# A pipelined two-block transformer on one core: the expert table read into registers at once, loads in pieces, and new orders

## What is computed

```python
h = layernorm(x) * (1 + ca) + sa
x = x + ga * attention0(h)                      # softmax(Q K^T / sqrt(128)) V
h = layernorm(x) * (1 + cb) + sb
x = x + gb * fp4_linear(silu(fp4_linear(h, w_gate)) * fp4_linear(h, w_up), w_down)
h = layernorm(x) * (1 + ca1) + sa1
x = x + ga1 * attention1(h)                     # 16 heads, causal
h = layernorm(x) * (1 + cb1) + sb1
logits = h @ gate_w.T; weights = softmax(logits of the 4 experts); top 2, made to sum to 1
y = silu(h @ w1[e]) * (h @ w3[e]) @ w2[e]       # for each chosen expert e
x = x + gb1 * sum of weight[e] * y
```

## Time and profile before

| | |
|---|---|
| median of three runs | 1883.6 us (1878.56 to 1885.53) |
| the profiled execution | 1871.67 us, span 1869.9 us |
| instructions | 39385 |
| ScalarE, GpSimd busy | 753.6 us (40%), 764.6 us (41%) |
| weight loads on TensorE | 1179.5 us (63%) |
| transfers | 291.39 MB, mean 156 GB/s |
| mean granted TensorE clock | 0.88 |

### The profile page before, as it was taken

How to read it: one execution, slowest core, us unless ns; L and a number is a source line. 1 busy time by engine, 2 the same in 40 slices (tenths; PEclk the granted TensorE clock), 3 DMA queues, 4 the chain that set the end, 5 groups by cost and what they waited for, 6 DMA issues and landing times. The chain is left out here.

```text
span 1869.9 us, 39385 instructions
## 1 busy us (share of the span) xinstructions
PE 1493.6 (80%) x11729; PEld 1179.5 (63%) x11729; DVE 1244.7 (67%) x2855; ACT 753.6 (40%) x1627; POOL 764.6 (41%) x1324
## 2 busy tenths in 40 slices
PE   3447777898989898988898988899898888772665
PEld 2334544576767676767676777777676767572654
DVE  5567757595959596967787686868695935241332
ACT  1322635454445453535362636363545342320111
POOL 1000142445454545452626163636354545254332
PEclk7667969898999998999999899999898988785887
DMA  5232312464747473736373655556464746444566
GB/s 189 76 107 78 105 60 91 140 209 118 235 120 233 117 235 107 245 93 186 124 215 135 168 175 162 190 143 203 114 226 110 232 136 217 130 123 129 168 197 190
DMA packets 205191, 291.39 MB, mean 156 GB/s; under 512 B 35840, under 2 KB 167936, under 8 KB 200864
## 3 DMA queue, kind: packets, MB, share of 16 engines
q1 hardware_dynamic: 172176, 251.01, 41.1%
q0 software_dynamic: 25824, 27.74, 7.6%
q10 hardware_dynamic: 7088, 11.29, 1.7%
HBM read 215.26 MB, written 70.91 MB: 153 GB/s over the span
## 5 line engine op out<-in xcount | busy, mean ns | idle before, releaser
L938 POOL DMA_INDIRECT acc<-ys,blk x134 | 219.1, 1635 | 448.7 <-issue 249.2
L1804 PE MATMUL bank<-xs_hi,wring 128*128 128x256 f32 x804 | 272.2, 339 | 68.7 <-DVE mneg L1455 30.6
L1455 DVE TENSOR_REDUCE mneg<-bank 128x2 f32<-128x512 f32 (+1 forms) x384 | 238.1, 682 | 60.2 <-remote 41.5
L1125 ACT ACTIVATE arena<-bank 128x512 f32<-128x512 f32 x384 | 197.9, 601 | 133.9 <-PE bank L1691 132.6
L1820 PE MATMUL y_ps<-wring,h 128*128 128x128 f32 (+1 forms) x1608 | 236.8, 289 | 8.3 <-DVE h L1516 7.5
L1805 PE MATMUL bank<-xs_hi,wring 128*128 128x256 f32 x804 | 239.6, 298 | 0.0
L1806 PE MATMUL bank<-xs_lo,wring 128*128 128x256 f32 x804 | 239.4, 298 | 0.0
L1804 PEld LDWEIGHTS bank<-xs_hi,wring 128*128 128x128 f32 x804 | 165.5, 206 | 100.8 <-issue 38.4
L1820 PEld LDWEIGHTS y_ps<-wring,h 128*128 128x128 f32 (+1 forms) x1608 | 207.5, 196 | 26.6 <-DVE h L1516 8.3
L798 POOL TENSOR_TENSOR rstd_a<-ve_a,mhalf 128x4 f32<-128x4 f32 x48 | 49.3, 1027 | 379.0 <-DVE ve_a L1334 376.5
L1516 DVE TENSOR_TENSOR h<-tt,bank 128x512 f32<-128x512 f32 x201 | 134.6, 681 | 71.3 <-PE bank L1806 66.3
(11 more groups left out here) (249 smaller groups left out, 3028.9 us busy)
## 6 DMA issues: line engine op xcount, KB each, us to landing
wring<-w_all SPq DMA_DIRECT2D x201, 640.0 KB, 6.7
blk<-queue SPq DMA_DIRECT2D x67, 272.0 KB, 2.8
q_stack<-q_rows SPq DMA_DIRECT2D x16, 1024.0 KB, 8.7
k_stack<-k_rows SPq DMA_DIRECT2D x16, 1024.0 KB, 11.0
rows<-mod_rows SPq DMA_DIRECT2D x32, 384.0 KB, 3.8
q_rows<-qk_halves SPq DMA_DIRECT2D x48, 256.0 KB, 5.5
k_rows<-qk_halves SPq DMA_DIRECT2D x48, 256.0 KB, 5.6
w_all<-wring ACTq DMA_DIRECT2D x4, 1536.0 KB, 6.5
```

Source lines behind the costliest of these rows:

```text
L938: send(g.indirect_dma_start(acc, bass.IndirectOffsetOnAxis(ap=blk[:, b, t, IDCOL:IDCOL + 1].bitcast(I32), axis=0), ys[:, b % 2, t, :], Non ...
L1125: frees(a(prob(u, g), ps.bank(use)[:], ACT.Exp, scale=SCALE1), use)
L1455: frees(v.tensor_reduce(dst, ps.bank(use)[:].rearrange("p (h k) -> p h k", k=P if name[0] == "A" else S), AX, ALU.max, negate=True), use)
L1804: mm(dst[:, at], w_hi[:, w], xs_hi[:, b % 2, :], start=True, stop=False)
```

## The change

`blocks(it)` and `weights(it, u)` no longer read the table. A new step of SyncE, `read`, waits for the table, reads its eight entries into registers one after another and then releases the table with a semaphore of its own, `table_read`; `make_table` waits for that and no longer for the landing of the ten kinds of loads. `blocks` loads one block, so its four parts can stand at different places of SyncE's list. `weights` and `blocks` build their addresses from the registers. All five orders and the row of bank uses are made anew; the same steps occur as before, some of them for another lead. Of the orders the new lines are shown, and the old ones of SyncE and GpSimd (the old ones of the others stand above); of `USES` only its first line.

```diff
@@ -80,101 +80,102 @@
 LOOP_AT, LOOPS = 2, 10
 
 
-MOE = ("gate", "up", "down", "swish", "times", "weights", "blocks", "table", "lift", "weigh_rows", "add_rows")
-
-
-USES = [(0, "eg1", "D", 5, 0, 4), (0, "eu0", "D", 6, 0, 5), (1, "OT1", "D", 4, 1, 2), (3, "G0", "D", 3, 3, 1),
...
+MOE = ("gate", "up", "down", "swish", "times", "weights", "read", "blocks", "table", "lift", "weigh_rows", "add_rows")
...
+USES = [(3, "G0", "D", 2, 3, 1), (3, "G1", "D", 6, 3, 2), (3, "U0", "D", 1, 3, 3), (0, "X1", "D", 4, 0, 3),
...
 def sp_order(do):
-    do(4, "load1"), do(0, "blocks"), do(0, "weights", 3), do(2, "store_q"), do(0, "weights", 4), do(2, "store_k")
-    do(0, "weights", 5), do(1, "turn_att"), do(0, "weights", 6), do(0, "weights", 7), do(0, "weights", 8), do(2, "stack")
-    do(0, "weights", 9), do(0, "weights", 10), do(1, "store3"), do(0, "weights", 11), do(2, "load4"), do(2, "stack_max")
-    do(4, "load2"), do(2, "stack_v"), do(2, "load3"), do(1, "weights", 0), do(1, "weights", 1), do(1, "weights", 2)
+    do(4, "load1"), do(1, "load3"), do(0, "read"), do(0, "blocks", 0), do(0, "weights", 0), do(0, "weights", 1)
+    do(0, "blocks", 1), do(0, "weights", 2), do(0, "weights", 3), do(2, "store_q"), do(0, "weights", 4), do(2, "store_k")
+    do(1, "turn_att"), do(0, "blocks", 2), do(0, "weights", 5), do(0, "weights", 6), do(2, "stack"), do(2, "stack_v")
+    do(0, "weights", 7), do(0, "blocks", 3), do(0, "weights", 8), do(0, "weights", 9), do(1, "store3"), do(2, "load4")
+    do(0, "weights", 10), do(2, "stack_max"), do(4, "load2"), do(0, "weights", 11)
 def pool_order(do):
-    do(4, "stats1"), do(0, "add_rows", 0), do(1, "stats4"), do(1, "modulate4"), do(1, "route"), do(0, "add_rows", 1)
-    do(1, "scatter"), do(1, "table"), do(3, "stats3"), do(4, "stats2"), do(0, "add_rows", 2), do(0, "add_rows", 3)
+    do(4, "stats1"), do(1, "stats4"), do(0, "add_rows", 0), do(1, "modulate4"), do(1, "route"), do(1, "scatter")
+    do(3, "stats3"), do(1, "table"), do(4, "stats2"), do(0, "add_rows", 1), do(0, "add_rows", 2), do(0, "add_rows", 3)
 def act_order(do):
...
+    do(3, "gate0", 1), do(0, "lift", 1), do(1, "weigh", 2), do(1, "weigh", 3), do(1, "turn_att"), do(4, "norm1")
+    do(3, "gate0", 2), do(3, "gate0", 3), do(0, "gate", 2), do(4, "turn1"), do(0, "gate", 3), do(2, "value1"), do(1, "norm4")
+    do(0, "lift", 2), do(0, "gate", 4), do(1, "turn4"), do(0, "gate", 5), do(1, "logits"), do(4, "query0"), do(4, "key0")
+    do(0, "gate", 6), do(3, "turn_h", 0), do(3, "turn_h", 1), do(3, "turn_h", 2), do(1, "ranks_out"), do(4, "scores0", 0)
+    do(3, "turn_h", 3), do(4, "scores0", 1), do(2, "carry"), do(0, "gate", 7), do(2, "turn_max"), do(4, "probs0", 0)
+    do(0, "gate", 8), do(0, "lift", 3), do(4, "probs0", 1), do(0, "gate", 9), do(0, "gate", 10), do(3, "norm3"), do(3, "turn3")
+    do(2, "rows", 0), do(2, "rows", 1), do(2, "rows", 2), do(2, "weigh", 0), do(4, "norm2"), do(0, "gate", 11)
+    do(2, "weigh", 1), do(2, "rows", 3), do(2, "rows", 4), do(1, "lift", 0), do(2, "rows", 5), do(3, "query1"), do(3, "key1")
+    do(1, "gate", 0), do(4, "turn2"), do(1, "gate", 1), do(4, "gate0", 0)
 def dve_order(do):
...
+    do(0, "swish", 0), do(4, "stats1"), do(0, "swish", 1), do(3, "gate0", 0), do(3, "gate0", 1), do(3, "up0", 0)
+    do(0, "lift", 1), do(3, "up0", 1), do(3, "quantise_h", 0, 0), do(1, "turn_out", 2), do(0, "times", 0), do(1, "turn_out", 3)
+    do(3, "quantise_h", 0, 1), do(0, "times", 1), do(3, "quantise_h", 0, 2), do(3, "gate0", 2), do(0, "swish", 2)
+    do(3, "gate0", 3), do(3, "up0", 2), do(0, "times", 2), do(1, "add3"), do(1, "stats4"), do(0, "swish", 3), do(3, "up0", 3)
+    do(0, "weigh_rows", 0), do(3, "quantise_h", 1, 0), do(0, "times", 3), do(0, "lift", 2), do(0, "swish", 4)
+    do(3, "quantise_h", 1, 1), do(4, "value0"), do(0, "times", 4), do(1, "logits"), do(0, "swish", 5), do(3, "quantise_h", 1, 2)
+    do(0, "times", 5), do(0, "swish", 6), do(2, "maxima", 0), do(0, "times", 6), do(2, "maxima", 1), do(2, "maxima", 2)
+    do(4, "scores0", 0), do(2, "maxima", 3), do(2, "maxima", 4), do(4, "scores0", 1), do(2, "maxima", 5), do(0, "swish", 7)
+    do(3, "down0"), do(2, "turn_max"), do(0, "weigh_rows", 1), do(0, "lift", 3), do(0, "swish", 8), do(3, "stats3")
+    do(0, "times", 7), do(0, "times", 8), do(0, "swish", 9), do(4, "out0"), do(0, "times", 9), do(0, "swish", 10)
+    do(4, "stats2"), do(0, "weigh_rows", 2), do(0, "times", 10), do(0, "swish", 11), do(4, "modulate2"), do(4, "quantise_x", 0)
+    do(0, "times", 11), do(4, "quantise_x", 1), do(2, "turn_out", 0), do(1, "lift", 0), do(4, "quantise_x", 2)
+    do(2, "turn_out", 1), do(0, "weigh_rows", 3), do(3, "query1"), do(3, "key1")
 def pe_order(do):
...
+    do(3, "gate0", 0), do(3, "gate0", 1), do(3, "up0", 0), do(0, "lift", 1), do(3, "up0", 1), do(1, "weigh", 3)
+    do(1, "turn_out", 2), do(0, "up", 0), do(1, "turn_out", 3), do(0, "up", 1), do(1, "turn_att"), do(3, "gate0", 2)
+    do(3, "gate0", 3), do(0, "gate", 2), do(0, "up", 2), do(3, "up0", 2), do(4, "turn1"), do(0, "down", 0), do(0, "gate", 3)
+    do(3, "up0", 3), do(0, "up", 3), do(2, "value1"), do(0, "down", 1), do(0, "down", 2), do(4, "value0"), do(0, "gate", 4)
+    do(0, "lift", 2), do(4, "key0"), do(0, "up", 4), do(1, "turn4"), do(0, "down", 3), do(0, "gate", 5), do(1, "logits")
+    do(0, "up", 5), do(4, "query0"), do(0, "gate", 6), do(2, "maxima", 0), do(3, "turn_h", 0), do(0, "up", 6)
+    do(2, "maxima", 1), do(3, "turn_h", 1), do(0, "down", 4), do(1, "ranks_in"), do(2, "maxima", 2), do(3, "turn_h", 2)
+    do(4, "scores0", 0), do(2, "maxima", 3), do(4, "scores0", 1), do(2, "maxima", 4), do(3, "turn_h", 3), do(0, "down", 5)
+    do(2, "maxima", 5), do(0, "gate", 7), do(3, "down0"), do(2, "turn_max"), do(4, "probs0", 0), do(0, "gate", 8)
+    do(0, "lift", 3), do(4, "probs0", 1), do(0, "up", 7), do(0, "up", 8), do(4, "out0"), do(0, "gate", 9), do(0, "gate", 10)
+    do(0, "down", 6), do(0, "up", 9), do(0, "down", 7), do(3, "turn3"), do(2, "rows", 0), do(2, "rows", 1), do(0, "down", 8)
+    do(2, "rows", 2), do(0, "up", 10), do(2, "weigh", 0), do(0, "gate", 11), do(2, "weigh", 1), do(2, "rows", 3)
+    do(0, "down", 9), do(2, "rows", 4), do(0, "up", 11), do(2, "turn_out", 0), do(2, "turn_out", 1), do(1, "lift", 0)
+    do(2, "rows", 5), do(0, "down", 10), do(3, "query1"), do(0, "down", 11), do(3, "key1"), do(1, "gate", 0), do(4, "turn2")
+    do(1, "gate", 1), do(2, "weigh", 2)
...
@@ -508,7 +509,7 @@
         place_ready, scattered = signal("place_ready", 1), signal("scattered", 2 * TILES, 16)
         step4 = signal("step4", 19)
 
-        table_ready, step5 = signal("table_ready", 1), signal("step5", 24)
+        table_ready, table_read, step5 = signal("table_ready", 1), signal("table_read", 1), signal("step5", 24)
         blk_loaded = [signal(f"blk_loaded{b}", 1, 16) for b in range(BLOCKS)]
         w_loaded = [signal(f"w_loaded{n}", STEPS // RING, 16) for n in range(RING)]
         xs_ready = signal("xs_ready", BLOCKS)
@@ -655,42 +656,47 @@
                 sp.wait_ge(x3_ready.sem, x3_ready.at(it, 1))
                 send(sp.dma_start(acc_v[bass.ds(it.scaled(1), 1)].rearrange("o t k d -> (o t) k d"), xb[:]), x3_stored)
 
-            def blocks(it):
-
-                if first_pair(it):
-                    sp.wait_ge(s_pads, 16 * PADROWS // SLOTS)
+            picks = {}
+
+            def read(it):
+
                 sp.wait_ge(table_ready.sem, table_ready.at(it, 1))
                 sp.sem_inc(s_past_sp, 1)
-                pair = enabling(it)
-                sp.wait_ge(scattered.sem, scattered.at(pair, 2 * TILES))
-                sp.sem_inc(s_past_sp, 1)
-                if it.reg is None and it.plus == GROUPS_MOE - 2:
-                    sp.wait_ge(s_flushed, 16 * 2 * EXP)
                 for b in range(BLOCKS):
-                    if it.reg is None and it.plus == GROUPS_MOE - 1 and UNITS * b >= LAST_STEPS:
-                        break
-                    if it.earlier():
-                        sp.wait_ge(added.sem, added.at(it.earlier(), 2 * b + 2))
-                        sp.sem_inc(s_past_sp, 1)
-                        sp.wait_ge(y_ready.sem, y_ready.at(it.earlier(), b + 1))
-                        sp.sem_inc(s_past_sp, 1)
-                    at = sp.value_load(table[0:1, b:b + 1], min_val=0, max_val=QROWS - SLOTS)
-                    send(sp.dma_start(blk[:, b], queue[bass.ds(at, SLOTS), :].rearrange("(t p) d -> p t d", p=P)), blk_loaded[b])
+                    picks["row", b] = sp.value_load(table[0:1, b:b + 1], min_val=0, max_val=QROWS - SLOTS)
+                for b in range(BLOCKS):
+                    picks["expert", b] = sp.value_load(table[0:1, BLOCKS + b:BLOCKS + b + 1], min_val=0, max_val=EXP - 1)
+                sp.sem_inc(table_read.sem, 1)
+                table_read.sent += 1
+
+            def blocks(it, b):
+
+                if first_pair(it) and b == 0:
+                    sp.wait_ge(s_pads, 16 * PADROWS // SLOTS)
```

(24 more changed lines are left out.)

41 lines of the change are left out of this document (2 added, 39 removed), and 56 rows, old and new, of the table USES.

## The result

The changed kernel takes 1894.6 us (median of 16 runs, 1889.3 to 1902.7), the kernel before in the same series 1880.8 us (16 runs): a ratio of 1.0092, 95% interval 1.0068 to 1.0117. It is 0.9% slower. The forecast was 1816 us, with 1868 us as the upper end.

A forecast was written before the change was run, and what follows sets the result against it. VectorE's work and engine exchanges were taken to bound steady turns, the table and add chain the tail. Gains of 37 us (turns) and 31 us (tail) sum to 68, giving 1816 us from 1883.6, range 1770 to 1868 us.

The forecast's parts named there:

- two such turns: TensorE's loop: two turns of 102.5 us beside instruction transfers, kept as two in the changed kernel, sum left alone.
- the likeliest case: Whole kernel: both the turns and the tail gain, 1790 to 1845 us, chance 0.50.
- The steady turn: Repeated pipeline turn: 92.8 us against 95.9, 3.1 us less for each of 12 turns, 37 us.
- the wait for `q_stack`: TensorE at `rows 0`: more work behind `turn_max` covers the transfer, so the 3.5 us wait goes.
- the gone gap of 5.8 us: VectorE at `out0`: it no longer stands behind the `q_stack` wait, so its 5.8 us gap goes.
- The stall beside the scatters: Last sets of maxima: late TensorE completions beside GpSimd's eight scatters stay, 4.0 to 5.7 us, counted as 5.3 us.
- the stall is hidden: Rival: scatters fall where TensorE is ahead, turns take 88 us, kernel 1758 us; chance 0.15.
- The release in the turns: GpSimd's table in steady turns: it is early already, so allowing it sooner is worth nothing.
- The tail: Stretch behind the last turn: 31 us less, from 20 us to 45 us as ends.
- the step of the chain of adds: Tail: one block's add pair to the next takes 8.2 us, 13 such steps giving 106.6 us.
- two of the three gaps: Tail: the earlier release removes two of TensorE's three waits for `blk`, 20.4 us of 58.0 us.
- GpSimd as the bound: Rival: GpSimd's unbroken row sets the turn, 3.5 us of adds unhidden each turn, kernel 1895 us; chance 0.09.

The follow-up runs named there:

- moved by 40 instructions: Changed kernel with 40 do-nothing semaphore increments at the head of TensorE's program: 0.976 of before, 1818.5 us. The kernel before, moved likewise: 1.012.
- moved by 100: Kernel before with 100 do-nothing semaphore increments at the head of TensorE's program: 0.996 of the unmoved kernel before, 1804.4 us.
- moved by 90: Changed kernel with 90 do-nothing semaphore increments at the head of TensorE's program: 0.981 of before, 1775.8 us; repeated at 0.979.
- the small loads: Changed kernel moved by 40, weight loads of groups 14 to 16 cut to 64 of 1280 columns (wrong results): 0.965 of before.
- both reorderings: Changed kernel moved by 40, on GpSimd either the first add pair ahead of stats4 (0.998 of before) or the next table behind stats2 (1.017).

## Why the prediction was wrong, point by point

**The instruction fetch: the step that failed.** The prediction saw the two turns of 102.5 us and the instruction transfers beside them, and kept "two such turns" for the changed kernel. It took for a property of the program what hangs on the place of a loop in its pages. The new orders put 15 instructions more ahead of TensorE's loop, and nine turns were fetched anew: 70.0 us on one chip, against some 13 us for the two turns that were counted in. This alone turns the sign: moved by 40 instructions the same kernel is at 0.976 of before. The prediction also misread the packets. It said that the eight other turns of the old loop stand without instruction transfers; in the trace the two long turns have six packets each, the two turns behind them three each, and two more have three at the loop's entry and exit, so that four of ten have none. A rival for the place of the loop was missing altogether: a kernel with 61 instruction packets for a program of some 43 pages is one whose loop sits at the edge, and 9 x 7 us stood to be lost or 2 x 7 us to be won.

In spans the forecast was 68 us less and the measurement 18.0 us more, 86 us apart: the loop's ten turns account for 91 us (59.9 more instead of 31 less) and the tail for 15 us; the two turns behind the loop gave 14 us and the start up to it 5 us more than forecast. Of the loop's 91 us, 57 are the fetches and 31 the gain of the orders that didn't come. Without the fetches the kernel (0.976 to 0.981 of before) would lie inside the stated range, but that would have been luck: the ten turns gained nothing, the tail half of what was forecast, and the rest comes from the start, the two turns behind the loop and the two fetches of the kernel before, where little or nothing was counted. By its own terms the likeliest case also reaches down to 1784 us and not to 1790.

**The steady turn: mechanism partly right, result wrong.** Forecast 92.8 us, from VectorE's 75.2 us of work, 12.3 us of gaps and 5.3 us beside the scatters. Without fetches the turn was 96.1 us: 76.4 us of work and 19.8 us idle. Right were the end of the wait for `q_stack`, the gone gap of 5.8 us, the gaps at `times 10` (1.7 us) and `swish 11` (3.5 us for 3.7), and the hidden add pair. Mis-sized were: work, by 1.2 us, since the multiplication in `quantise_h` (line 1245) takes 2.3 us more a turn beside the modulation than in the old order (the prediction booked the same loss as before); and idle time, by 2.2 us: `weigh_rows 2` waits 1.8 us and `times 11` 1.4 us for TensorE, which weren't on the list, while `swish 9` waits 0.9 us instead of 2.1. The wait at `up 5` was forecast as at most 2.1 us and took 4.5 us. So 3.1 us a turn, 37 us in all, came out as nothing in the loop; only the two turns behind it gained, 17.4 us.

**The stall beside the scatters.** The forecast kept it, and on the first chip it is there in the changed kernel too (VectorE waits up to 3.7 us for a releaser that isn't named). On the faster chips it isn't there in either kernel. In the kernel before moved by 100, VectorE's longest wait is the one at `out0` (line 1357), and at the maxima (line 1456) it waits 0.4 us at most, for TensorE:

```profile
DVE rinv L1357 <- PE bank L1635: 6.5, 1, 6.5
...
DVE mneg L1456 <- PE bank L1694: 0.5, 2, 0.4
```

and its turns are 91.5 instead of 95.9 us. The rival "the stall is hidden" thus described a chip and not the change.

**The release in the turns: wrong.** "In the steady turns this is worth nothing" held for the old orders. In the new ones SyncE's last weight loads land later, and the release is worth 6 us a turn. The cost of the reading in one piece was rightly called hidden for the new orders; in the old ones the run with reading and release together has turns some 2 us longer, and which of the two does it is not shown.

**The tail: mechanism right in the main, size off.** Forecast 31 us, measured 16.0 us. The tables of groups 15 and 16 were made while the groups before ran, and TensorE waited long for `blk` once (29.9 us; 33.5 us in all against 58.0). From the table of group 14 to the last pair took 128.8 us, forecast 119 and 115 to 125 as the test, before 145.8. The term that failed is the step of the chain of adds: 8.2 us, taken from the tail before, where an add landed after 4.5 us (in that kernel moved by 100). In the changed tail (moved by 90) it lands after 7.2 to 7.8 us, the steps between blocks 1 to 3 are 9.8 to 11.1 us, and the pair behind a table comes 13.9 us after the one before it. The 3.5 us for the pair of adds that left the way to the table of group 14 didn't show either: from the last `ranks_in` to that table it is 38.6 us, before 37.7. That the streaming weights hold this chain up, the small loads show: 17 us back. That the release "removes two of the three gaps" by itself is refuted by the run with the release alone, 61.5 us in three waits.

**The head** (0 to 324 us) was to stay within 5 us and became 8.2 us shorter (324.8 to 316.6 us). No run took it apart.

**GpSimd as the bound** didn't come true: its row reaches `stats2` just when VectorE delivers, and both reorderings of it made the turn longer. The time of this rival, 1895 us, is the measured one, by chance: its cause, 3.5 us of adds on the path of each turn, would have made turns of 99 us without a fetch, and they take 96.1 us.

## What to carry to other kernels

Before a reordering is judged, look at the instruction queues of both profiles: if a looped kernel moves more packets than its program has pages, some turns are fetched anew, and a few instructions more or less ahead of the loop are worth more than the orders. Some idle instructions at the head tell code placement from scheduling, at more than one count, since 40 helped one kernel here and harmed the other; so does the same kernel without a loop. An early release is worth what its next user can do with it: here it brought nothing under the old orders, and 6 us a turn plus 17 us at the end under the new ones. A step that hangs on a transfer, taken from a stretch in which the queues are less busy, is a lower end for one in which they are busier.

## What the runs showed of the hardware

- TensorE's loop of some 1587 instructions ran nine jumps back without one packet on its instruction queue wherever it touched seven pages of 16 KB, and with nine packets for each turn that was fetched anew where it touched eight. Such a turn is some 7.8 us longer in the changed kernel and 6 to 10 us in the kernel before, of which 4 to 6 us is the gap.
- VectorE shows the same on another queue, in packets of 8 KB: a loop of 337 instructions that grew by one and moved by two took that queue from 40 to 85 packets, five in each turn behind a jump, and put 3.5 to 4.4 us ahead of the loop's first work in a turn.
- A VectorE multiplication of 128x704 elements took 3.19 us beside GpSimd's modulation and 0.89 us in the kernel before moved by 100, where it runs without it; the two operations behind it 1.47 us for 0.53, as in the earlier trace rows. The Trainium skill, "SBUF — State Buffer", section "SBUF: two separate sides", has the two engines lock each other out of one shared pair of ports; the trace agrees in kind.
- The adds of the tail landed 3.3 us after their issue where the weight loads were small, 4.1 to 4.6 us in the kernel before (moved), and 7.2 to 7.8 us in the changed one (medians).
- Chips differ by 3 to 4% on one program (each was measured on one occasion only). Most of it is 4 us a turn. On the slower ones waits stand beside the scatters (4.0 us in the kernel before, 2.2 us in the changed one moved by 40, and 2.4 us at a `swish` behind them); on the three faster ones VectorE has no wait of this kind in the loop, in any run of either kernel. What makes a chip do so is open.
